# Perceiver layer on one core: weighted values of two steps in one burst, and each block's part turned and joined inside the loop

## The reference, cut to what matters

```
q = layernorm(x) @ Wq.T + bq           # 128 x 256, scaled by 0.25
k = ctx @ Wk.T + bk                    # 12544 x 256
v = ctx @ Wv.T + bv
scores = einsum('bhqd,bhkd->bhqk', q, k)
attn = softmax(scores, axis=-1)        # over the 12544 keys
x = x + (einsum('bhqk,bhkd->bhqd', attn, v) as 128 x 256) @ Wo.T + bo
x = x + linear_attention(layernorm(x)) # gate, feature map, k^T v
x = x + causal_attention_and_experts(layernorm(x))
```

## Time and profile before

| | us |
|---|---|
| median of three runs | 589.88 |
| the runs | 588.37, 589.88, 593.8 |
| the profiled execution, its own time | 590.74 |
| its span in the profile | 588.9 |
| sweep with key loads and weighted values, about | 68.9 to 437 |
| scores and weighted values of the last steps | to 483.0 |
| the two other attentions and the experts | from 489.0 to the end |

### The profile page before, as it was taken

One profiled execution on the slowest core, in us unless ns is written; L12 is line 12 of the kernel. 1 busy time (PEld: TensorE's weight loads), 2 busy tenths in 40 slices (PEclk: granted clock), 3 DMA queues, 4 the chain that ended last, 5 costly groups with the idle time before them and its releaser, 6 DMA issues.

```text
span 588.9 us, 15872 instructions
## 1 busy us (share of the span) xinstructions
PE 555.1 (94%) x6517; PEld 512.9 (87%) x6517; DVE 423.2 (72%) x804; ACT 331.6 (56%) x636; POOL 91.5 (16%) x75
## 2 busy tenths in 40 slices
PE   7778999999999999999999999999998998878797
PEld 7677899999999999999999999999986887846686
DVE  5678787787787787777787877877875237876674
ACT  3322666576676676676666666766766650052463
POOL 7551111111101101101101111011000000006000
PEclk9888999999999999999999999999999999988899
DMA  5999887768768778768678687785375009920000
GB/s 183 135 144 143 144 192 114 126 119 120 121 118 124 117 116 127 117 111 128 119 113 128 118 117 120 118 126 98 78 110 170 3 27 376 375 82 1 1 0 9
DMA packets 44651, 70.46 MB, mean 120 GB/s; under 512 B 6788, under 2 KB 15140, under 8 KB 44452
## 3 DMA queue, kind: packets, MB, share of 16 engines
q1 hardware_dynamic: 44580, 69.47, 64.1%
HBM read 30.56 MB, written 0.13 MB: 52 GB/s over the span
## 4 chain that ended last, share of the span: by engine, by line
PE 79%; DVE 7%; DMA 7%; SPq 3%; ACT 2%; issue 2%; DVEq 0%; ACTq 0%
PE bank L589 16%; PE bank L605 15%; PE bank L565 15%; PE bank L533 11%; PE bank L548 10%; DMA kT<-kst 5%; PE bank L805 3%; SPq L242 3%; PE bank L821 2%; PE bank L613 1%; DMA ctxT<-in_ctxT 1%; PE bank L626 1%; DVE stepmax L917 1%; DMA qmat<-maxT 1%; PE bank L518 1%
## 5 line engine op out<-in xcount | busy, mean ns | idle before, releaser
L917 DVE TENSOR_REDUCE stepmax<-bank 128x2 f32<-128x512 f32 x392 | 263.4, 688 | 98.8 <-PE bank L565 76.3
L391 ACT ACTIVATE probs<-bank 128x512 f32<-128x512 f32 x392 | 226.9, 602 | 146.3 <-PE bank L589 144.9
L565 PE MATMUL bank<-kT,qM 128*128 128x256 f32 x784 | 166.3, 294 | 8.5 <-DMA kT<-kst 7.1
L589 PE MATMUL bank<-qmat,kT 128*128 128x256 f32 x784 | 162.8, 292 | 4.3 <-DMA kT<-kst 1.7
L589 PEld LDWEIGHTS bank<-qmat,kT 128*128 128x128 f32 x784 | 120.2, 191 | 17.6 <-issue 10.1
L565 PEld LDWEIGHTS bank<-kT,qM 128*128 128x128 f32 x784 | 123.0, 194 | 14.2 <-DMA kT<-kst 7.0
L314 POOL TENSOR_TENSOR cparts<-ctxT,cparts 128x512 fp32r<-128x512 f32 x49 | 62.7, 1279 | 338.4 <-ACT cparts L361 338.4
L533 PE MATMUL bank<-cparts,wk 128*128 128x256 f32 x588 | 104.2, 288 | 1.9 <-DVE kst L901 1.9
L548 PE MATMUL bank<-wv,cparts 128*128 128x256 f32 x588 | 101.9, 284 | 0.7 <-ACT val L381 0.7
L605 PE MATMUL bank<-probs,val 128*17 128x128 f32 x3136 | 95.1, 273 | 0.0
L533 PEld LDWEIGHTS bank<-cparts,wk 128*128 128x128 f32 x588 | 86.2, 196 | 2.3 <-POOL cparts L314 2.3
(11 more groups left out here) (188 smaller groups left out, 324.9 us busy)
## 6 DMA issues: line engine op xcount, KB each, us to landing
kT<-kst SPq DMA_DIRECT2D x294, 128.0 KB, 4.6
ctxT<-in_ctxT SPq DMA_DIRECT2D x49, 256.0 KB, 5.3
w<-in_w SPq DMA_DIRECT2D x24, 512.0 KB, 10.1
bias<-in_biases SPq DMA_DIRECT2D x1, 1024.0 KB, 5.9
qmat<-maxT SPq DMA_DIRECT2D x26, 8.0 KB
w_xk<-in_w_xk SPq DMA_DIRECT2D x1, 256.0 KB, 3.4
w_xq<-in_w_xq SPq DMA_DIRECT2D x1, 256.0 KB, 3.5
bias<-in_biases SPq DMA_DIRECT2D x1, 256.0 KB, 6.0
```

Source lines behind the costliest of these rows:

```text
L391: act.activation(probs[k % PROBS][:, :, :], sc_bank[k % 3][:, :].rearrange("p (h q) -> p h q", q=P), ACT.Exp).then_inc(S["exp_ready"], 1)
L565: last = pe.matmul(mx_bank[p % 2][:, a * SK:(a + 1) * SK], qM[:, p, a, :], kT[:, n % RING, p, :], start=True, stop=True)
L589: last = pe.matmul(sc_bank[k % 3][:, i * 2 * P:(i + 1) * 2 * P], kT[:, n % RING, p, j * P:(j + 1) * P], qmat[b % 2][:, p, :, :], start=Tru ...
L917: dve.tensor_reduce(stepmax[:, n % BS, 2 * p:2 * p + 2], mx_bank[p % 2][:, :].rearrange("p (a k) -> p a k", a=2), AX_X, ALU.max).then_inc( ...
```

## The change

Weighted values run only in every second pass (odd t, at q = 1), for two steps at once; the last step is alone. The exponentials get 20 buffers and the values' ring 10 places. `kT` keeps its 7 places. In place of all blocks' parts one `part` is kept, and `sm` and `kbd` of the later stages move to other addresses.

The maximum is now a running one: `stepmax` has one more row, which holds the maximum so far, and `block_max` takes it along. At q = 3 of the pass after a block's last step VectorE takes the difference of old and new maximum (`fade_diff`) and keeps the new one (`keep_running`); ScalarE takes its exponential at q = 5 (`fade_out`). At q = 6 of pass last_step(b) + 5 VectorE multiplies `merged` with that factor (`fade_joined`). A block's part is copied out by ScalarE at q = 2 as before, turned at q = 3 of the same pass by four transposes of TensorE back into `pv_bank`, and added to `merged` at q = 5 of that pass (`join`); the next block's weighted values wait for `joined`. Of what followed the loop only a wait for the last `joined` is left. The selection matrix goes.

```diff
-VRING = 8
+VRING = 10
-PROBS = 12
+PROBS = 20
...
             def part_out(b):
                 act.wait_ge(S["pv_done"], 2 * last_step(b) + 2)
-                act.activation(parts[:, b, :], pv_bank[:, :], ACT.Copy).then_inc(S["part_ready"], 1)
+                if b >= 1:
+                    act.wait_ge(S["pe_partT"], b)
+                act.activation(part[:, :], pv_bank[:, :], ACT.Copy).then_inc(S["part_ready"], 1)
+            def fade_out(b):
+                act.wait_ge(S["fade_diff"], b)
+                if b >= 3:
+                    act.wait_ge(S["faded"], b - 2)
+                act.activation(fade[:, b % 2, :], fade[:, b % 2, :], ACT.Exp).then_inc(S["fade_ready"], 1)
...
+                    if q == 5:
+                        for b in range(1, NB):
+                            if t == last_step(b) + 1:
+                                fade_out(b)
...
                 if first and b > 0:
-                    pe.wait_ge(S["part_ready"], b)
+                    pe.wait_ge(S["joined"], b)
...
             def turn_part(b):
                 pe.wait_ge(S["part_ready"], b + 1)
...
-                    last = pe.matmul(B[b % 2][:, g * GH * VW:(g + 1) * GH * VW], parts[:, b, g * P:(g + 1) * P],
-                                     const[:, C_SEL:C_SEL + GH * VW], start=True, stop=True)
+                    last = pe.transpose(pv_bank[:, g * P:(g + 1) * P], part[:, g * P:(g + 1) * P], ident)
...
-                    if q == 1 and 0 <= n - 1:
-                        weighted_values(n - 1, 0)
-                        weighted_values(n - 1, 1)
-                    if t > NS and q % 4 == 3 and 2 * (t - NS - 1) + q // 4 < NB - 3:
-                        turn_part(2 * (t - NS - 1) + q // 4)
-            for b in range(NB - 3, NB):
-                turn_part(b)
+                    if q == 1 and 0 <= n - 1 and ((n - 1) % 2 == 1 or n == NS):
+                        for m in range((n - 1) // 2 * 2, n):
+                            weighted_values(m, 0)
+                            weighted_values(m, 1)
+                    if q == 3:
+                        for b in range(NB):
+                            if n - 1 == last_step(b):
+                                turn_part(b)
...
+                if b >= 1:
+                    dve.wait_ge(S["run_kept"], b)
+                dve.tensor_reduce(curmax[:, :], stepmax[:, (0 if b else 1):1 + count, :].rearrange("p s h -> p h s"),
+                                  AX_X, ALU.max).then_inc(S["curmax_ready"], 1)
...
-                dve.tensor_scalar(bmax[:, b, :], curmax[:, :], 1.0, None, ALU.mult).then_inc(S["bmax_ready"], 1)
+            def fade_diff(b):
+                if b >= 3:
+                    dve.wait_ge(S["faded"], b - 2)
+                dve.tensor_tensor(fade[:, b % 2, :], stepmax[:, 0, :], curmax[:, :], ALU.subtract
+                                  ).then_inc(S["fade_diff"], 1)
+            def keep_running(b):
+                if b >= 1:
+                    dve.wait_ge(S["fade_diff"], b)
+                dve.tensor_scalar(stepmax[:, 0, :], curmax[:, :], 1.0, None, ALU.mult).then_inc(S["run_kept"], 1)
+            def fade_joined(b):
+                dve.wait_ge(S["fade_ready"], b)
+                dve.wait_ge(S["joined"], b)
+                dve.tensor_tensor(merged, merged, per_head(fade[:, b % 2, :], VW), ALU.mult).then_inc(S["faded"], 1)
+            def join(b):
+                dve.wait_ge(S["pe_partT"], b + 1)
+                turned_part = pv_bank[:, :].rearrange("p (h v) -> p h v", v=P // GH)[:, :, 0:VW]
+                if b == 0:
+                    dve.tensor_copy(merged, turned_part).then_inc(S["joined"], 1)
+                else:
+                    dve.wait_ge(S["faded"], b)
+                    dve.tensor_tensor(merged, merged, turned_part, ALU.add).then_inc(S["joined"], 1)
...
+                    if q == 3:
+                        for b in range(NB - 1):
+                            if t == last_step(b) + 1:
+                                if b >= 1:
+                                    fade_diff(b)
+                                keep_running(b)
...
+                    if q == 4 and t == NS:
+                        fade_diff(NB - 1)
+                    if q == 6:
+                        for b in range(1, NB):
+                            if t - LAG == last_step(b):
+                                fade_joined(b)
+                    if q == 5:
+                        for b in range(NB):
+                            if t - LAG - 1 == last_step(b):
+                                join(b)
...
-            for b in range(NB):
-                dve.wait_ge(S["pe_partT"], b + 1)
-                bank = B[b % 2][:, 0:H * VW].rearrange("p (h v) -> p h v", v=VW)
-                ins = dve.tensor_tensor(merged if b == 0 else piece, bank, per_head(bmax[:, b, :], VW), ALU.mult)
-                ins.then_inc(S["dve_partT_read"], 1)
-                dve.wait_ge(S["dve_partT_read"], b + 1)
-                if b:
-                    link(dve.tensor_tensor(merged, merged, piece, ALU.add))
+            dve.wait_ge(S["joined"], NB)
```

More of the change, by code:

```diff
@@ L44 @@
 C_ID, C_BM, C_CA, C_HM, C_LT = 0, 128, 256, 384, 392
-C_SEL = C_LT + EXPERTS * EXPERTS
-C_N = C_SEL + GH * VW
+C_N = C_LT + EXPERTS * EXPERTS
 def block_of(n):
@@ L74 @@
     "mparts_ready",
-    "bmax_ready",
+    "fade_diff",
+    "run_kept",
+    "fade_ready",
+    "faded",
+    "joined",
     "mt_done",
@@ L89 @@
     "dve_xn", "pe_xnT", "dve_xnT", "pe_q", "dve_qparts", "pe_qT", "dve_q0", "act_q0",
-    "dve_dmax", "act_bw", "pe_partT", "dve_partT_read",
+    "pe_partT", "dve_partT_read",
     "dve_att", "pe_attT", "dve_attT", "pe_xo",
@@ L121, in perceiver_layer @@
         ones = sb("ones", [P, 1])
-        bmax = sb("bmax", [P, NB, H])
+        fade = sb("fade", [P, 2, H])
         small = sb("small", [P, 512])
@@ L127, in perceiver_layer @@
         xnT = sb("xnT", [P, DC, P])
-        stepmax = sb("stepmax", [P, BS, H])
+        stepmax = sb("stepmax", [P, BS + 1, H])
         curmax = sb("curmax", [P, H])
@@ L161, in perceiver_layer @@
         kst = [place(f"kst{i}", [P, 2, 2 * SK], F32R) for i in range(2)]
-        parts = place("parts", [P, NB, GROUPS * P])
+        part = place("part", [P, GROUPS * P])
         parts_start = temps_start + 2 * 4096
@@ L186, in perceiver_layer @@
         pT = place("pT", [P, H, P])
+        sm = place("sm", [P, H, P])
+        kbd = place("kbd", [P, DC, H // DC, P])
         assert at[0] <= tail_start
@@ L191, in perceiver_layer @@
         tc = place("tc", [P, 2 * D])
-        sm = place("sm", [P, H, P])
-        kbd = place("kbd", [P, DC, H // DC, P])
         oT = place("oT", [P, GROUPS, P])
@@ L432, in _ @@
                         keys_high(t + 2)
-                    if t == NS + 1 and q == 2:
-                        act.wait_ge(S["dve_dmax"], 1)
-                        act.activation(bmax[:, :, :], bmax[:, :, :], ACT.Exp).then_inc(S["act_bw"], 1)
+                    if q == 5:
+                        for b in range(1, NB):
+                            if t == last_step(b) + 1:
+                                fade_out(b)
             act.wait_ge(S["dve_a_neg"], 1)
@@ L916, in step_max @@
                 dve.wait_ge(S["mx_done"], 8 * n + p + 1)
-                dve.tensor_reduce(stepmax[:, n % BS, 2 * p:2 * p + 2],
+                dve.tensor_reduce(stepmax[:, 1 + n % BS, 2 * p:2 * p + 2],
                                   mx_bank[p % 2][:, :].rearrange("p (a k) -> p a k", a=2), AX_X, ALU.max
@@ L945, in _ @@
             dve.memset(warm[:, :], 0.0).then_inc(S["dve_warm"], 1)
+            merged = merged_t[:, :].rearrange("p (h v) -> p h v", v=VW)
             dve.memset(pv_bank[:, :], 0.0).then_inc(S["dve_pvzero"], 1)
@@ L985, in _ @@
                                 max_turned(b)
+                    if q == 3:
[4 more added lines that the diff above has]
+                                keep_running(b)
                     if q == 5 and t + 2 < NS:
                         keys_low(t + 2)
-            dve.wait_ge(S["ld_small"], 64)
-            dve.wait_ge(S["bmax_ready"], NB)
-            link(dve.tensor_reduce(small[:, 16:32], bmax[:, :, :].rearrange("p b h -> p h b"), AX_X, ALU.max))
-            dve.tensor_tensor(bmax[:, :, :], bmax[:, :, :], over_heads(small[:, 16:32], NB), ALU.subtract
-                              ).then_inc(S["dve_dmax"], 1)
-            dve.wait_ge(S["act_bw"], 1)
-            merged = merged_t[:, :].rearrange("p (h v) -> p h v", v=VW)
-            piece = small[:, 224:224 + H * VW].rearrange("p (h v) -> p h v", v=VW)
-            for b in range(NB):
-                dve.wait_ge(S["pe_partT"], b + 1)
-                bank = B[b % 2][:, 0:H * VW].rearrange("p (h v) -> p h v", v=VW)
-                ins = dve.tensor_tensor(merged if b == 0 else piece, bank, per_head(bmax[:, b, :], VW), ALU.mult)
-                ins.then_inc(S["dve_partT_read"], 1)
-                dve.wait_ge(S["dve_partT_read"], b + 1)
-                if b:
```

(7 more changed lines are left out.)

9 lines of the change are left out of this document (removed).

## The result

The changed kernel takes 616.95 us (median of 4 runs, 612.31 to 618.11), against 591.84 for the kernel before on the same chip: a ratio of 1.0432, 95% interval 1.0381 to 1.0483. The forecast was 611, range 598 to 626. The profiled execution has a span of 614.8 us (588.9 before).

The account below looks back on a forecast made before the run. TensorE bounds the sweep, key loads close behind. Terms +21.0 (load stalls), -1.5, +5.0 (turned parts), +4.0 (max_rows), +0.2 (steps 46 to 49), -7.5 (end) sum to +21.2 on 590.74: 611.9, less 0.9 for the median, 611 us; range 598 to 626.

Parts of the forecast that it names:

- Sum and size: Sweep, t = 5 to 45: key-load stalls +21.0 us, less 1.5 for waits absorbed, turned parts +5.0, max_rows +4.0.
- A: Start of the scores of q = 7 in an odd step t; times after it are in us.
- The sign that I had named: TensorE's scores wait about 1.4 us for key copies in some 20 odd steps, near 28 us in all.
- Merges, 0.31 each: TensorE's weighted values: each merge of two bursts saves 0.31 us, the double burst taking 3.62.
- The step that failed: Key copies, gated by q = 7 scores, land at A + 9.2; short step needs them at A + 7.83: 1.4 us stall.
- VectorE at 0: VectorE's added work in the sweep costs 0 while key loads stall; upper bound 0.5 us in 10 block steps.
- max_rows, 0.4: Maxima's copies, queued behind key copies on SP, land late at block steps: 0.4 us in 10 blocks, bounds 0 to 0.9.
- Turned parts, 0.5: Four transposes per block after the double burst cost TensorE 0.5 us, bounds 0.4 to 0.9; ten blocks +5.0.
- The end, -7.5: After the last key load, burst of t = 49 to reciprocal: 28.9 us instead of 36.4, bounds -5 to -9.
- The clock (645): Rival: TensorE's clock falls in the new stalls, 1.7 us each by 20, +34; 645 us, chance 0.05.
- Faster (582): Rival: no long key wait, VectorE catches up in the double burst, -9; 582 us, chance 0.07.
- rival 1: Key loads land 1.3 us sooner and VectorE binds instead, +8; 599 us, chance 0.10.

Follow-up runs that it names:

- all places moved: Changed kernel plus ring of 8, early keys, turn_max and max_turned at q = 3, fades outside the block's step: 602.65 us with bursts of two, 589.28 single.
- Ring of 8 alone: Changed kernel with 8 instead of 7 places for turned keys, paid for with fewer exponential and value buffers: 617.81 us, ratio 1.0406.
- both together: Changed kernel with ring of 8 and keys_high, keys_low each one slot earlier (q = 3 and 4): 597.91 us, ratio 1.0103.
- the one run that was to try it: Changed kernel with scores one step further behind the keys, ring of 8, and keys computed one slot earlier: 614.69 us, ratio 1.0417.
- these two runs: Bursts of two, ring of 8, early keys, fades moved: turn_max and max_turned at q = 3 (602.65 us), or at q = 1 with values copied before block maximum (600.78).
- VectorE's new order: Bursts of two, ring of 8, early keys, fades moved; values' copy before block maximum, turn_max and max_turned at q = 1: 600.78 us, ratio 1.0167.
- LAG 6: Changed kernel with scores one step further behind the keys, ring of 8, VRING 10, PROBS 17: 620.38 us, ratio 1.0495.
- early keys alone: Changed kernel with keys_high at q = 3 and keys_low at q = 4, one slot earlier, ring still 7: 612.63 us, ratio 1.0368.

## Why the prediction was right, by its steps

- **Sum and size.** From t = 5 to 45 the terms gave +28.5; from A of t = 5 to A of t = 45 the kernel before takes 358.89 (from 65.59) and the changed one 453.44 - 64.32 = 389.12, so +30.2. Four steps took 38.62, by my terms 38.7. That this is so close is luck: the keys' copies cost 0.27 less in each pair (0.5 in four steps) and the maxima's 0.5 more than put down. Most of what the sweep lies above the terms is in three pairs, 19.59, 19.86 and 19.76 long instead of 19.1: in two of them the last keys' copy took 6.0 us, in the third an issue took 1.55 instead of 0.6. The sign that I had named, a wait of about 1.4 in some 20 steps and near 28 us in all, came as 11 waits and 9.5 us in the sweep. The rest: steps to t = 49 +0.5 (predicted +0.2), the end -5.4 (burst end 482.04 to the reciprocal at 513.06: 31.0) instead of -7.5; the start 1.3 us sooner, and 1.8 more after the reciprocal. The median lies 6 above the forecast: 2.1 from the end, 2.0 from the sweep with t = 46 to 49, 0.5 from start and rest, and the last 1.3 because I had taken off 0.9 for the profiled execution of before, which lay above its median, while that of the changed kernel lies 0.3 below.
- **Merges, 0.31 each.** The double burst takes 3.62, to the hundredth. But a pair without a stall gained 0.1 in the runs with all places moved; another 0.2 went there into one weight load's wait for the keys. What this merge saves is too small to pay for any wait. By the Trainium skill (TensorEngine Tiling (Array Packing), section Tiling Modes) a change of tiling mode drains the array. The 0.21 us of "issue" before the load behind each burst, here too, agrees with that.
- **The step that failed: who holds the keys' copies.** The prediction has "The ring has 7 places, so the keys of t+2 take the place of those of t-5", and takes the scores of q = 7 for the one gate of the copies. Place and size (A + 8.98 against A + 9.25) were right, the size in part by luck: the last issue began at A + 3.66, not A + 4.91, and its copy landed after 5.27, not 4.3. The cause was half: `keys_low` at q = 5 of VectorE ends at A + 0.49, the same moment. Ring of 8 alone (617.8) and both together (597.9) show it. SP's waits in the trace of before gave no hint, since only the later gate is named there. But the earlier trace rows did: `keys_low` ends at 262.60 + 0.87 = 263.47, which is 0.48 after q = 7 of that step (254.06 + 8.93), and the issue that I read from the earlier trace rows begins 0.51 after its q = 7.
- **VectorE at 0.** Right for the kernel as it is ("as long as the loads stall"), and the sum A + 8.9 for the block's step was close: behind the loads stood VectorE, as the later runs brought out. Missed was its effect inside the step: TensorE's turn_max waits 0.78 at 283.16 for the values' copy, ten times. In the pair with the block's end the landing of the maxima's copies sets the end of the pair, so this wait does not add to it.
- **max_rows, 0.4.** There (6.1 us in 10), and larger. The second issue began at A + 5.83, sooner than I had it, and its copy took 3.89, not 3.22; it landed at A + 9.72, within my A + 9.4 to 10.0. In the pair with the block's end it is the whole final stall, 0.5 to 0.9, and that pair took 19.55, where one with the keys' wait and without a turned part takes 18.64: 0.9, the upper bound.
- **Turned parts, 0.5.** 0.43: the four transposes take 0.35, and the slot behind them is 0.08 longer. The join does hold the max-scores of the next step, by 0.24 (261.63), but as I had it this is hidden behind the load: 18.64 without turns and joins and 0.43 already make the 19.07.
- **The end, -7.5.** I priced the steps at 11.7 and 11.0; the bursts are 12.3 and 11.1 apart (478.42, 490.73, 501.85). The first holds a wait of 0.83 for ScalarE's copy of the part and the chain behind it.
- **Rivals.** The clock (645): in the changed kernel's sweep the granted clock stayed 1.00, the 2.4 GHz level, through stalls of 0.5 to 1.4 us. What the Trainium skill tells of a transfer awaited in each tile (TensorE: Matmul & The Clock Gate, section HAM oscillation) did not come about in it. The rival was nearer than that looks: in the sweeps of three other merged kernels the clock did fall to its lower level, four times in all, behind longer waits. Faster (582): its condition, VectorE catching up in the double burst, is what the run with early keys and ring of 8 refutes: with the copies out in time the merged kernel is still 1% slower than before. Its 597.9 is near rival 1's number, 599, with the loads out of the way.

## What to carry to other kernels

A burst on the busiest engine is also a pause for the others: merging two moves the pause, and the step that loses it must hold all its helpers' work. Before merging, sum each helper's work for the step without the burst, block ends included: VectorE's 7.5 us did not fit into 6.87. Whether the pause, placed in the step with the largest sum, makes the merge pay is not shown; the one run that was to try it still had a gate closed. When a transfer is late, look for a second gate that opens at the same moment, by the critical chain of a window and not by the queue's waits alone: an experiment that opens one of two shows nothing. Look in the trace of before too: an operation that ends just when a queue starts may be a gate, whether or not the waits name it.

## What was unexpected of the hardware

The six keys' copies took 8.4 us from first issue to last landing (260.65 to 269.08), 5.27 of them from the start of the last issue. A pair of 8 KB copies landed 3.79 us after the start of its second issue when the queue had taken nothing for 1.4 us (from 238.73 to 240.15), and 4.58 when it came right behind the copies of keys and context. The other block ends of these two runs go the same way, by the end of TensorE's wait for the copy: with the gap of 1.4 us 3.3 to 4.9, in the middle 3.4; right behind the others 3.1 to 5.1, in the middle 4.5. In the changed kernel, also right behind, it is 3.9 to 4.4. So the queue's traffic goes with most of a microsecond for a small copy, about what VectorE's new order had won; no run varies the traffic alone.

The granted clock fell in the sweep (64 to 450 us) in three of the 14 profiled executions, four times, each time to its lower level, 1.2 GHz, and within a microsecond of the end of a wait for a copy in which TensorE had done next to nothing: 1.95 us (ring of 8 alone), 2.42 (LAG 6), 2.52 and 1.96 (bursts of two with all places moved). It did not fall behind one of 2.03 us (early keys alone), nor behind any wait of 1.8 us or less. Behind the three that ended a pair with a block's maximum the pair was 2.2 to 3.0 us longer than the usual one, 1.1 to 1.6 of it the longer wait; with the wait of 2.03 and no fall it was 1.5 longer, all of it the wait. An estimate from these: a fall costs 1.1 to 1.4 us here. A stall that grows by a microsecond can so cost more than that microsecond.
